# Step times per kind of batch: other places for a second half's projections and gates, a norm, a score maximum and the next batch's input

## The chip, the cores and the metric

The kernel runs on one core of a Trainium2 chip. The metric is the device time of one execution in microseconds; the median of three runs is compared. On the core, five engines work side by side, each through its own fixed list of instructions: TensorE (PE in the profile, its weight loads PEld), VectorE (DVE), ScalarE (ACT), GpSimd (POOL), and SyncE (SP), which issues transfers. They meet only at semaphores.

## The reference

Four batches of 1024 tokens of width 128 pass through four stages, each followed by a residual sum and a layer norm:

```python
x = _layernorm(x + _L0_attn_ref(x, ...))   # 8 heads, silu, rotary-like angles, exp mask, rms norm, gate
x = _layernorm(x + _L0_ffn_ref(x, ...))    # 2 layers: window attention over 64+64 keys, then gelu feed-forward
x = _layernorm(x + _L1_attn_ref(x, ...))   # 33 interpolated samples per token at computed positions, weighted
x = _layernorm(x + _L1_ffn_ref(x, ...))    # 8 experts, top 2 of a softmax over the tokens
```

The third stage computes, for each token, a frequency and a phase from two small projections (`wave`), 33 positions `pos`, and sums the rows at `floor(pos)` and the next one with weights from a third projection (`kernel`).

## The kernel before

A batch has a **first half** (the first two stages) and a **second half** (the third). The second half of batch b runs beside the first half of batch b+1, woven into it, and the experts' stage runs beside and behind the second half of batch 3. Everything in 128-token tiles t = 0 to 7 or in blocks j = 0, 1 of 512 tokens. In float32 a matmul shows as two records in the profile.

The first half's steps, by the names that `first` knows: the **opening** (`xT` transposes the loaded input, `kq` 0 to 7 are key and query projections with a Silu on ACT and a rotation on DVE, then `vu`, `kt`, `u`, `KV`, four pairs `E`/`heads` of masked scores, `square`, `rms`, `y`, `ao`, and the norms `mean`/`var` 0 and 1), then for two layers and eight tiles `proj`, `rn`, `rot`, `turn`, `v`, `S` (scores; on DVE their maximum), `X` (exp), `P`, `O`, `oT`, and by block `wo`, `mean`/`var`, three `ff` steps (gate and up projections, Gelu on ACT, product on DVE), and `down`. `shift` copies a block with half of its channels moved by a token. Norms 6 and 7 close the first half of blocks 0 and 1. So `ff(1,1,0)`, `ff(1,1,1)`, `ff(1,1,2)`, `down(1,1)`, `var(7)` are its last steps.

The second half: `x2t` j transposes the block, which SP writes to a table in memory, `wk` t is the projection of tile t, `pos` j the positions and gates of a block (on ACT a Silu, a Sigmoid and a Tanh with the tables that they need; on DVE eleven small instructions); `w` weights, then 88 chunks `g`: POOL gathers three times 128 rows, DVE multiplies them by weights (L1235), PE sums them by transposing into a bank (`acc`, L1612). Six chunk buffers go round. `wk` 4 to 7, `x2t` 1 and `co` share the one bank `c1`; `xT`, `kq`, norms, projections and feed-forward take turns in the two banks `pa` and `pb`, in program order.

What sets the order: no planner runs; `schedule(e)` writes each engine's list by **sorting the steps by a time**, a table value plus the batch's offset (`FIRST_AT`, `SECOND_AT`, a batch every 27.61 units) and a phase of the engine (`AT`). PE's list is also that of SP and POOL. A step in front that waits holds all behind it on that engine. The input of batch b+1 is loaded by SP in its `xT` step (L630), behind the store of the second half's last block (L658), which waits for DVE's `co` 1.

```python
def schedule(e):
    out = []
    for b in range(B):
        out += [(FIRST_AT[b] + time, ("first", b, *step)) for time, step in first_times(e)]
        out += [(SECOND_AT[b] + time, ("second", b, *step)) for time, step in second_times() if b < B - 1 or time < TAIL_AT]
    return [step for _, step in sorted(out, key=lambda x: x[0])] + tail_steps()
```

Of the kernel before, what the change touches and what calls it, by code (L numbers as in the profile page):

```python
# [79 lines left out]
FIRST_AT = (0.0, 27.61, 55.22, 82.83)  # L80
SECOND_AT = (0.0, 27.61, 55.22, 82.83)
TAIL_AT = 21.94
SECOND_LAYER = 9.0
OPENING_AT = (-10.02, -8.96, -8.18, -7.82, -7.49, -7.26, -7.09, -6.96, -6.78, -6.42, -6.24, -6.23, -5.49, -4.17, -3.83, -3.72, -3.41, -3.27, -3.2, -2.79, -2.78, -2.77, -2.76, -2.75, -2.49, -2.42, -2.27, -2.26, -2.25, -2.24, -2.23, -2.22, -2.19, -2.18, -2.13, -0.83)
DENSE_AT = ((5.59, 5.61, 5.89, 6.03, 6.23, 6.61), (9.33, 9.57, 9.81, 9.82, 10.54, 10.77), (14.63, 14.84, 15.16, 15.84, 16.08, 16.75, 17.15, 17.74), (18.22, 18.4, 18.45, 19.2, 19.51, 19.63, 20.16, 20.81))
HEAD_AT = ((17.93, 17.99, 18.0, 18.13, 18.14, 18.21, 19.38), (21.23, 21.24, 22.92, 23.7, 24.34, 25.36))
CHUNK = (0, 8, 9, 30, 45, 60, 75, 88)
CHUNK_AT = (19.61, 21.76, 23.16, 28.75, 33.26, 37.56, 41.27, 45.64)
SUM_LAG = 0.42
AT = {  # L90
# [9 lines left out]
def norm_steps(m):  # L100
    return [("mean", m), ("var", m)]


# [4 lines left out]
def opening_steps():

    steps = [("zero",), ("xT",)] + [("kq", i) for i in range(2 * J * G)] + [("vu",), ("kt",), ("u",), ("KV",), ("E", 0), ("E", 1), ("heads", 0), ("E", 2), ("heads", 1)]  # L110
    steps += [("square", 0), ("E", 3), ("heads", 2), ("rms", 0), ("heads", 3), ("y", 0), ("square", 1), ("ao", 0), ("rms", 1), ("mean", 0), ("y", 1), ("var", 0), ("ao", 1)]
    return steps + [("mean", 1), ("shift", 0, 0), ("var", 1), ("shift", 0, 1)]


def first_times(e):

    at = AT[e]
    out = [(time + at["opening"], step) for time, step in zip(OPENING_AT, opening_steps())]
    for l in range(LAYERS):
        for what, phase in at.items():  # L120
            if what not in ("wo", "opening", "dense"):
                out += [(SECOND_LAYER * l + t + phase, (what, l, t)) for t in range(T)]
        for j in range(J):
# [113 lines left out]
def tail_steps():  # L237

    late = second_head(1)
    done = {step for time, step in second_times() if time < TAIL_AT}  # L240
# [24 lines left out]
    return [("moe", B, "load")] + second[:h] + merge(second[h:k], [("moe", B, *x) for x in beside]) + second[k:] + [("moe", B, *x) for x in behind]  # L265
# [1578 lines left out]
```

## Time and profile before

| | |
|---|---|
| median of 3 runs (lowest to highest) | 1969.92 us (1968.27 to 1970.03) |
| the profiled execution, span | 2353.6 us |
| mean granted TensorE clock in it | 0.854 |
| busy: PE, DVE, ACT, POOL | 1720.4, 1254.1, 988.0, 1103.7 us |
| one batch's period | some 512 us |

The profiled execution has no time of its own beside its span, which begins with the first instruction and ends with the last. It took 1.195 times the median of the runs, so a time read from it stands for 0.837 of that in a run, if the stretch is like the rest. Starts are in microseconds from the span's start. A wait in square brackets is the idle time of the engine ahead of the instruction and who ended it.

### The profile page before, as it was taken

How to read it: one execution, taken by the hardware profiler on the slowest of the kernel's cores; microseconds unless marked ns; L12 is line 12 of the kernel's file. 1: busy time of each engine (PE TensorE's matmuls, PEld its weight loads, DVE VectorE, ACT ScalarE, POOL GpSimd, SP SyncE). 2: the span in 40 equal slices, each digit the busy share in tenths (PEclk: the TensorE clock that was granted, in tenths of full speed). 3: DMA queues.
4: the chain of work that ended last, by engine and by line, in shares of the span. 5: the costliest groups of instructions: out<-in, count | busy, mean ns of one | idle time of the engine just before them, and what ended most of it. 6: DMA issues, size and time to landing. Idle time of an engine off the chain costs nothing.

```text
span 2353.6 us, 31786 instructions
## 1 busy us (share of the span) xinstructions
PE 1720.4 (73%) x12145; PEld 1141.7 (49%) x12153; DVE 1254.1 (53%) x2158; ACT 988.0 (42%) x2363; POOL 1103.7 (47%) x1069
## 2 busy tenths in 40 slices
PE   5787876767777766666776766667787768879866
PEld 3354534445445534344555434454455346656645
DVE  6565645555556444555565545655565454343345
ACT  3365673234543551243353540335354533343333
POOL 0000016475556345664556255554665367766630
PEclk8799998778989877988898978789888879989876
DMA  3010023132223232232223232232233343223321
GB/s 133 10 24 14 19 48 96 58 102 83 79 75 103 63 74 79 79 96 73 88 79 90 56 95 70 83 90 72 86 89 85 69 148 99 88 81 90 88 47 36
DMA packets 93420, 178.72 MB, mean 76 GB/s; under 512 B 21452, under 2 KB 50264, under 8 KB 93016
## 3 DMA queue, kind: packets, MB, share of 16 engines
q0 software_dynamic: 50688, 138.48, 21.4%
q1 hardware_dynamic: 42584, 38.23, 5.8%
q8 instruction: 98, 1.61, 0.3%
q14 instruction: 50, 0.41, 0.1%
HBM read 151.46 MB, written 9.44 MB: 68 GB/s over the span
## 4 chain that ended last, share of the span: by engine, by line
PE 39%; DVE 19%; another core or an unknown queue 18%; ACT 12%; issue 9%; SPq 1%; POOL 1%; DMA 1%; DVEq 0%; POOLq 0%; ACTq 0%
PE c L1612 5%; DVE pool_c L1235 4%; PE pa L1508 3%; PE pb L1508 3%; PE ta L1542 2%; DVE ssq L1132 2%; PE ta L1516 2%; ACT pool_a L771 2%; ACT pool_a L836 2%; PE sc L1587 2%; DVE pool_a L1155 1%; DVE pool_a L1185 1%; PE tb L1389 1%; PE pb L1560 1%
## 5 line engine op out<-in xcount | busy, mean ns | idle before, releaser
L729 POOL DMA_INDIRECT pool_c<-rows_of_x,idx x1056 | 1100.9, 1043 | 1156.5 <-PE c L1612 380.0
L1612 PE MATMUL c<-ident,pool_c 128*128 128x128 f32 x2112 | 337.1, 303 | 61.6 <-DVE pool_c L1235 32.2
L1612 PEld LDWEIGHTS c<-ident,pool_c 128*128 128x128 f32 x2112 | 278.3, 158 | 143.0 <-issue 97.0
L1235 DVE TENSOR_TENSOR pool_c<-pool_c 128x768 f32<-128x768 f32 x352 | 331.3, 951 | 20.1 <-DMA pool_c<-rows_of_x,idx 19.7
L860 ACT ACTIVATE prob<-sc,nmax 128x128 f32<-128x128 f32 x512 | 179.3, 374 | 0.1
L1516 PE MATMUL ta<-ident,pool_a 128*128 128x128 f32 x512 | 90.9, 333 | 90.8 <-DVE pool_a L1155 80.4
L771 ACT COPY pool_a<-tb 128x512 f32<-128x512 f32 x188 | 112.5, 599 | 103.6 <-remote 58.3
L1155 DVE TENSOR_TENSOR pool_a<-ta,rinv 128x512 f32<-128x512 f32 x64 | 44.3, 692 | 199.9 <-remote 158.3
L1542 PE MATMUL ta<-vmix,pool_a 128*64 128x64 f32 x1024 | 80.9, 239 | 81.0 <-ACT pool_a L771 67.5
L1142 DVE TENSOR_REDUCE nmax<-sc 128x8 f32<-128x1024 f32 x64 | 77.5, 1211 | 103.9 <-remote 96.1
L1508 PE MATMUL pa<-wqkv,pool_a 128*128 128x512 f32 x192 | 118.8, 706 | 12.9 <-DVE pool_a L1185 7.4
L1516 PEld LDWEIGHTS ta<-ident,pool_a 128*128 128x128 f32 x512 | 74.6, 173 | 108.5 <-DVE pool_a L1155 87.6
L1508 PE MATMUL pb<-wqkv,pool_a 128*128 128x512 f32 x192 | 115.5, 687 | 13.3 <-DVE xm L1160 6.3
L1542 PEld LDWEIGHTS ta<-vmix,pool_a 128*64 128x64 f32 x1024 | 73.0, 152 | 101.7 <-issue 101.7
L860 ACT ACTIVATION_READ_ACCUMULATOR prob<-sc,nmax 128x1 f32 x512 | 109.8, 214 | 0.0
L836 ACT ACTIVATE pool_a<-pb 128x512 f32<-128x512 f32 x64 | 38.2, 597 | 168.7 <-PE pb L1508 100.1
L836 ACT ACTIVATE pool_a<-pa 128x512 f32<-128x512 f32 x64 | 38.2, 597 | 164.9 <-PE pa L1508 100.5
L1132 DVE TENSOR_REDUCE ssq<-pool_a 128x16 f32<-128x1024 f32 x64 | 77.9, 1218 | 43.9 <-ACT pool_a L836 42.0
L1542 PE MATMUL ta<-vring,pool_a 128*64 128x64 f32 x1024 | 82.3, 241 | 0.0
L1516 PE MATMUL tb<-ident,pool_a 128*128 128x128 f32 x512 | 77.8, 299 | 4.5 <-issue 4.4
L1199 DVE TENSOR_TENSOR pool_a<-pool_a,rot 128x1024 f32<-128x1024 f32 x64 | 78.4, 1225 | 2.2
L1196 DVE TENSOR_TENSOR pool_a<-pool_a,rot 128x1024 f32<-128x1024 f32 x64 | 78.1, 1220 | 2.8 <-remote 2.2
(413 smaller groups left out, 3344.3 us busy)
## 6 DMA issues: line engine op xcount, KB each, us to landing
pool_c<-rows_of_x,idx POOLq DMA_INDIRECT x1056
vmix<-vring SPq DMA_DIRECT2D x128, 128.0 KB
rows_of_x<-x2tok SPq DMA_DIRECT2D x16, 256.0 KB
xtok<-in_x SPq DMA_DIRECT2D x4, 512.0 KB
x_of_all<-x2tok SPq DMA_DIRECT2D x8, 256.0 KB
out<-pool_c SPq DMA_DIRECT2D x8, 256.0 KB, 2.3
wqkv<-in_wqkv SPq DMA_DIRECT2D x1, 1536.0 KB
xtok<-x_of_all SPq DMA_DIRECT2D x3, 512.0 KB
```

The costliest lines, as they stand in the source:

```text
L729: pool.indirect_dma_start(gat[:, n % GB, s, :], None, tables[b % 2], bass.IndirectOffsetOnAxis(ap=idx[:, t, SC * c + s:SC * c + s + 1], ax ...
L771: nc.scalar.copy(dst, src[:, :] if view is None else view(src)).then_inc(empty(key, b), 1)
L836: nc.scalar.activation(sq[:, w, :], src[:, :], ACT.Square).then_inc(SEM["b_square"], 1)
L860: ins = nc.scalar.activation(prob[:, n % 2, pr, e, :], sc[:, e, P * pr:P * (pr + 1)], ACT.Exp, bias=nmax[:, n % 2, e, pr:pr + 1], accum_ou ...
L1132: V.tensor_reduce(ssq[:, t % 2, 0, :], sq[:, :, :].rearrange("p w (h d) -> p (w h) d", h=HB), AXX, ALU.add).then_inc(SEM["b_ss"], 1)
L1196: V.tensor_tensor(r2.rearrange("p w h (s d) -> p w h s d", s=2), bass.AP(tensor=own.tensor, offset=own.offset + 32, ap=[own.ap[0], [INNER, ...
L1199: V.tensor_tensor(own.rearrange("p w (h d) -> p w h d", h=HB), own.rearrange("p w (h d) -> p w h d", h=HB), ap3(rot[:, l, t, 0, 0, :], [[D ...
L1235: V.tensor_tensor(g4, g4, wv, ALU.mult).then_inc(SEM["c_prod"], 1)
L1508: mm(out[:, :], hT[:, P * n:P * (n + 1)], wqkv[:, l, c:c + INNER], start=True, stop=True).then_inc(full(key, b), 1)
L1516: ins = mm(out[:, P * (k % PAIRS):P * (k % PAIRS + 1)], x, ident[:], start=(k == 0), stop=(k == len(parts) - 1), is_transpose=True, skip_g ...
L1542: ins = mm(out[q, DH * (2 * pr + e):DH * (2 * pr + e + 1)], PT[:, n % 2, pr, e, q], v[:, 2 * pr + e, :], start=True, stop=True, skip_group ...
L1612: ins = mm(out[:, c:c + P], x, ident[:], start=(i == 0 and k == 0), stop=(i == BCH - 1 and k == len(parts) - 1), is_transpose=True, skip_g ...
```

## The change

The tables get one version for each kind of batch: `KIND` sends batch 0 to version 0, batches 1 and 2 to version 1, batch 3 to version 2. Only times change, so each engine executes the same steps; ACT loads its function tables four times less (112 loads instead of 116). SP and POOL have the same lists as before. The diff, cut (`OPENING_AT`, `DENSE_AT` and `CHUNK_AT` have a row for each kind as `HEAD_AT` has):

```diff
@@
-HEAD_AT = ((17.93, 17.99, 18.0, 18.13, 18.14, 18.21, 19.38), (21.23, 21.24, 22.92, 23.7, 24.34, 25.36))
+KIND = (0, 1, 1, 2)
...
+HEAD_AT = (
+    ((17.93, 17.99, 18.0, 18.13, 18.14, 18.21, 19.38), (21.23, 21.24, 22.31, 25.46, 25.96, 26.48)),
+    ((17.93, 17.99, 18.0, 18.13, 18.14, 18.21, 19.31), (20.95, 21.17, 22.31, 25.46, 26.02, 26.34)),
+    ((17.93, 17.99, 18.0, 18.13, 18.14, 18.21, 19.38), (20.96, 21.23, 22.31, 25.46, 26.02, 26.31)),
+)
...
-    "pe": {"dense": 0.01, "proj": -1.95, "P": 1.06, "O": 1.27, "turn": -0.55, "v": -0.28, "oT": 1.72, "opening": -0.14, "S": -0.12, "wo": 1.9},
+    "pe": {"dense": 0.01, "proj": -1.95, "P": 1.06, "O": 1.24, "turn": -0.55, "v": -0.28, "oT": 1.72, "opening": -0.14, "S": -0.14, "wo": 1.91},
...
-def first_times(e):
+def first_times(e, b):
...
-    out = [(time + at["opening"], step) for time, step in zip(OPENING_AT, opening_steps())]
+    out = [(time + at["opening"], step) for time, step in zip(OPENING_AT[KIND[b]], opening_steps())]
...
-def second_times():
+def second_times(b):
...
-        out += list(zip(HEAD_AT[j], second_head(j)))
+        out += list(zip(HEAD_AT[KIND[b]][j], second_head(j)))
```

The numbers of the second row of `HEAD_AT` are the times of `x2t` 1, `wk` 4 to 7 and `pos` 1. Lines of the changed file from `tail_steps` on are 18 higher.

**PE, end of the first half of batch 1 and start of batch 2.** Before: `var(5)` (L1501), `ff(1,1,0)` (two of L1560), `xT` (two of L1389), `ff(1,1,1)`, `kq` 0 (L1405), `ff(1,1,2)`, `down(1,1)` (L1569), `kq` 1.

```order
L1501 MATMUL pa<-lnq,meanw 128x512
L1560 MATMUL pb<-pool_a,w 128x512
L1560 MATMUL pa<-pool_a,w 128x512
L1389 MATMUL pb<-ident,xtok 128x128 x4
L1389 MATMUL pa<-ident,xtok 128x128 x4
L1560 MATMUL pb<-pool_a,w 128x512
L1560 MATMUL pa<-pool_a,w 128x512
L1405 MATMUL pb<-xin,wkq 128x512
L1560 MATMUL pa<-pool_a,w 85x512
L1560 MATMUL pb<-pool_a,w 85x512
L1569 MATMUL pa<-up,w 128x512 x3
L1405 MATMUL pb<-xin,wkq 128x512
```

The same place in the change:

```order
L1519 MATMUL pa<-lnq,meanw 128x512
L1407 MATMUL pb<-ident,xtok 128x128 x4
L1407 MATMUL pa<-ident,xtok 128x128 x4
L1578 MATMUL pb<-pool_a,w 128x512
L1578 MATMUL pa<-pool_a,w 128x512
L1578 MATMUL pb<-pool_a,w 128x512
L1578 MATMUL pa<-pool_a,w 128x512
L1578 MATMUL pb<-pool_a,w 85x512
L1578 MATMUL pa<-pool_a,w 85x512
L1423 MATMUL pb<-xin,wkq 128x512
L1587 MATMUL pa<-up,w 128x512 x3
L1423 MATMUL pb<-xin,wkq 128x512
```

`xT` has moved ahead of all three `ff` steps and `kq` 0 behind them; it is so between batches 2 and 3 too, and not between 0 and 1. ACT's and DVE's lists follow. Behind this piece, `var(7)` moves from behind `kq` 6 to behind `kq` 3 on PE, and `x2t` 1 and `wk` 4 to ahead of `vu`.

**DVE, opening of batch 2.** Before: the last product of mask and scores (L1065) of `E` 0, a chunk product (L1235), `wk` 6 (L1213), the four of `E` 1, two chunk products.

```order
L1065 TENSOR_TENSOR pool_a<-tb,emask 128x512
L1235 TENSOR_TENSOR pool_c<-pool_c 128x768
L1213 TENSOR_TENSOR pool_c<-c,cb 128x280
L1065 TENSOR_TENSOR pool_a<-pa,emask 128x512
L1065 TENSOR_TENSOR pool_a<-pb,emask 128x512
L1065 TENSOR_TENSOR pool_a<-ta,emask 128x512
L1065 TENSOR_TENSOR pool_a<-tb,emask 128x512
L1235 TENSOR_TENSOR pool_c<-pool_c 128x768 x2
```

In the change:

```order
L1083 TENSOR_TENSOR pool_a<-tb,emask 128x512
L1253 TENSOR_TENSOR pool_c<-pool_c 128x768
L1083 TENSOR_TENSOR pool_a<-pa,emask 128x512
L1083 TENSOR_TENSOR pool_a<-pb,emask 128x512
L1083 TENSOR_TENSOR pool_a<-ta,emask 128x512
L1083 TENSOR_TENSOR pool_a<-tb,emask 128x512
L1253 TENSOR_TENSOR pool_c<-pool_c 128x768
```

`wk` 6 is gone from here and each chunk product stands one `E` earlier (the second one of the pair did). On PE, `wk` 6 leaves its place behind `E` 0, `wk` 7 its place behind `heads` 1, and the sums `acc` 10 and 11 move ahead of `E` 1. All three openings of batches 1 to 3 have it.

**ACT, norms and first projection of batch 2.** Before: `var(0)` (L823, L825), `pos` 1 of batch 1 with three table loads (L894 to L767), `mean(1)` (L818), `var(1)`, `proj` (L836).

```order
L823 ACTIVATE lnq<-pa,cols 128x512
L825 ACTIVATE lnq<-lnq 128x512
L894 ACT_TABLE_LOAD
L894 ACTIVATE pool_c<-pool_c 128x1120
L896 ACT_TABLE_LOAD
L896 ACTIVATE pool_c<-pool_c 128x32
L897 ACTIVATE pool_c<-pool_c 128x32
L767 ACT_TABLE_LOAD
L818 ACTIVATE lnq<-lnc 128x512
L823 ACTIVATE lnq<-pb,cols 128x512
L825 ACTIVATE lnq<-lnq 128x512
L836 ACTIVATE pool_a<-pa 128x512
```

In the change:

```order
L836 ACTIVATE lnq<-lnc 128x512
L854 ACTIVATE pool_a<-pb 128x512
L854 ACTIVATE pool_a<-pa 128x512
L860 ACTIVATE ssq<-ssq 128x16
L862 ACTIVATE ssq<-ssq,cols 128x16
L841 ACTIVATE lnq<-pb,cols 128x512
L843 ACTIVATE lnq<-lnq 128x512
L912 ACT_TABLE_LOAD
L912 ACTIVATE pool_c<-pool_c 128x1120
L914 ACT_TABLE_LOAD
L914 ACTIVATE pool_c<-pool_c 128x32
L915 ACTIVATE pool_c<-pool_c 128x32
```

`mean(1)`, the projection's squares and `rn` now stand ahead, then `var(1)`, then `pos` 1. On DVE `pos` 1 moves from between `shift(0,0)` and `var(1)` to behind `rot(0,0)`, `shift(0,1)` from behind `proj(0,1)` to behind `rot(0,1)`, and `wk` 6 and 7 stand between the first tile's steps. For batch 3, ACT has `pos` 1 ahead of `var(1)`.

Elsewhere, in the second layer, DVE has a chunk product ahead of some score maxima (tiles 1 to 3) that stood behind them, and PE and ACT have the tile-6 `P` ahead of `ff(1,0,1)`. In all, 59 chunk products stand ahead of a step of the first half that stood ahead of them.

## Rows read from the trace of the kernel before

**Rows 1.** The page: span, busy time of each engine, chain that ended last.

```profile
span 2353.6 us, 31786 instructions
...
PE 1720.4 (73%) x12145; PEld 1141.7 (49%) x12153; DVE 1254.1 (53%) x2158; ACT 988.0 (42%) x2363; POOL 1103.7 (47%) x1069
...
PE 39%; DVE 19%; another core or an unknown queue 18%; ACT 12%; issue 9%; SPq 1%; POOL 1%; DMA 1%; DVEq 0%; POOLq 0%; ACTq 0%
...
L1235 DVE TENSOR_TENSOR pool_c<-pool_c 128x768 f32<-128x768 f32 x352 | 331.3, 951 | 20.1 <-DMA pool_c<-rows_of_x,idx 19.7
```

**Rows 2.** All waits: engine, line, released by: us in total, times, longest.

```profile
POOL pool_c L729 <- PE c L1612: 380.0, 104, 13.8
...
DVE pool_a L1155 <- remote: 158.3, 35, 6.5
...
DVE pool_c L1235 <- DMA pool_c<-rows_of_x,idx: 19.7, 7, 4.7
```

**Rows 3.** Timeline, batches 1 to 2: start, us, engine, line, tiles, [idle before <- releaser].

```profile
844.38 0.51 SPq L630 DMA_DIRECT2D xtok<-in_x  x1
...
846.79 0.72 ACT L828 ACTIVATE pool_a<-lnc,cols 128x512 f32<-128x512 f32 x1 [0.82 <-DVE lnc L1113]
...
853.34 0.70 PE L1389 MATMUL pb<-ident,xtok 128*128 128x128 f32 x4 [2.40 <-DMA xtok<-in_x]
...
858.61 0.75 DVE L1166 SCALAR_TENSOR_TENSOR up<-pa,cols,lnq 128x512 f32<-128x512 f32 x1 [6.88 <-PE pa L1560]
...
862.84 1.28 ACT L880 ACT_TABLE_LOAD   x1
...
864.24 0.68 ACT L880 ACTIVATE lnc<-pa,cols 85x512 f32<-85x512 f32 x1
...
865.91 5.28 PE L1569 MATMUL pa<-up,w 128*128 128x512 f32 x6 [1.95 <-DVE up L1166]
```

**Rows 4.** Timeline, the same place between batches 2 and 3.

```profile
1364.65 0.66 PE L1389 MATMUL pa<-ident,xtok 128*128 128x128 f32 x4 [1.85 <-DMA xtok<-in_x]
...
1377.88 2.90 PE L1569 MATMUL pb<-up,w 128*128 128x512 f32 x3 [4.06 <-DVE up L1166]
```

**Rows 5.** The six down matmuls alone: stretch, us, PE busy, PEld busy, PEclk, DMA.

```profile
865.80:872.00 6.20, 5.28 (x6) 1.85 (x6) 0.59 0.00 0
353.60:357.00 3.40, 2.81 (x6) 1.06 (x6) 1.00 0.54 122
```

**Rows 6.** Timeline, var(7) and the second half's transposes, batches 1 to 2.

```profile
884.95 0.69 DVE L1119 TENSOR_TENSOR xm<-lnc,lnq 128x512 f32<-128x512 f32 x1 [3.14 <-ACT lnq L825]
...
890.75 0.59 ACT L771 COPY x2tok<-c 128x512 f32<-128x512 f32 x1 [3.84 <-remote]
...
891.39 1.30 PE L1600 MATMUL c<-wc,xm 128*128 128x280 f32 x2 [2.37 <-ACT x2tok L771]
```

**Rows 7.** Timeline of PE and of DVE, the opening of batch 2.

```profile
925.76 0.55 PE L1446 MATMUL pa<-pool_a 32*128 32x128 f32 x1 [5.49 <-DVE pool_a L1065]
...
934.78 0.69 DVE L1065 TENSOR_TENSOR pool_a<-pa,emask 128x512 f32<-128x512 f32 x1 [2.65 <-PE pa L1446]
...
938.45 0.63 PE L1600 MATMUL c<-wc,xm 128*128 128x280 f32 x2 [1.01 <-issue]
```

**Rows 8.** Timelines of ACT, DVE and PE, first projection of batch 2.

```profile
965.04 0.63 ACT L818 ACTIVATE lnq<-lnc 128x512 f32<-128x512 f32 x1
...
964.67 0.22 DVE L1312 TENSOR_REDUCE pool_c<-pool_c 128x8 f32<-128x64 f32 x1
...
967.38 0.23 DVE L1323 TENSOR_SCALAR pool_c<-pool_c 128x132 f32<-128x132 f32 x1
...
968.87 1.52 PE L1508 MATMUL pa<-wqkv,pool_a 128*128 128x512 f32 x2
...
969.22 0.69 DVE L1111 TENSOR_TENSOR x<-lnc,lnq 128x512 f32<-128x512 f32 x1 [1.61 <-ACT lnq L825]
```

**Rows 9.** Timeline of DVE, a score maximum of the second layer.

```profile
1223.77 1.22 DVE L1142 TENSOR_REDUCE nmax<-sc 128x8 f32<-128x1024 f32 x1 [3.82 <-remote]
```

More of the change, by code:

```diff
@@ L83 @@
 SECOND_LAYER = 9.0
-OPENING_AT = (-10.02, -8.96, -8.18, -7.82, -7.49, -7.26, -7.09, -6.96, -6.78, -6.42, -6.24, -6.23, -5.49, -4.17, -3.83, -3.72, -3.41, -3.27, -3.2, -2.79, -2.78, -2.77, -2.76, -2.75, -2.49, -2.42, -2.27, -2.26, -2.25, -2.24, -2.23, -2.22, -2.19, -2.18, -2.13, -0.83)
-DENSE_AT = ((5.59, 5.61, 5.89, 6.03, 6.23, 6.61), (9.33, 9.57, 9.81, 9.82, 10.54, 10.77), (14.63, 14.84, 15.16, 15.84, 16.08, 16.75, 17.15, 17.74), (18.22, 18.4, 18.45, 19.2, 19.51, 19.63, 20.16, 20.81))
-HEAD_AT = ((17.93, 17.99, 18.0, 18.13, 18.14, 18.21, 19.38), (21.23, 21.24, 22.92, 23.7, 24.34, 25.36))
-CHUNK = (0, 8, 9, 30, 45, 60, 75, 88)
-CHUNK_AT = (19.61, 21.76, 23.16, 28.75, 33.26, 37.56, 41.27, 45.64)
+KIND = (0, 1, 1, 2)
+OPENING_AT = (
[3 rows of a table added]
+)
+DENSE_AT = (
[3 rows of a table added]
+)
+HEAD_AT = (
[3 rows of a table added]
+)
+CHUNK = (0, 8, 9, 30, 45, 60, 75, 88)
+CHUNK_AT = (
[3 rows of a table added]
+)
 SUM_LAG = 0.42
 AT = {
[1 row of a table removed]
[1 row of a table added]
     "act": {"dense": 0.12, "P": 1.17, "rn": -1.72, "X": 0.44, "turn": -0.48, "v": -0.17, "oT": 1.83, "opening": -0.06, "proj": -2.05},
[1 row of a table removed]
[1 row of a table added]
 }
@@ L128, in first_times @@
                 steps += norm_steps(6 + j)
-            out += [(time + at["dense"], step) for time, step in zip(DENSE_AT[J * l + j], steps)]
+            out += [(time + at["dense"], step) for time, step in zip(DENSE_AT[KIND[b]][J * l + j], steps)]
             if l == 0:
@@ L132, in first_times, with chunk_time @@
     return out
-def chunk_time(n):
+def chunk_time(b, n):
     k = max(i for i in range(len(CHUNK) - 1) if n >= CHUNK[i])
-    return CHUNK_AT[k] + (CHUNK_AT[k + 1] - CHUNK_AT[k]) * (n - CHUNK[k]) / (CHUNK[k + 1] - CHUNK[k])
-def second_times():
+    at = CHUNK_AT[KIND[b]]
+    return at[k] + (at[k + 1] - at[k]) * (n - CHUNK[k]) / (CHUNK[k + 1] - CHUNK[k])
+def second_times(b):
     lag = {"acc": SUM_LAG, "cT": SUM_LAG + 0.05, "co": SUM_LAG + 0.1}
@@ L145, in second_times @@
     for j in range(J):
-        out += list(zip(HEAD_AT[j], second_head(j)))
-    out.append((HEAD_AT[0][-1], ("w", 0)))
+        out += list(zip(HEAD_AT[KIND[b]][j], second_head(j)))
+    out.append((HEAD_AT[KIND[b]][0][-1], ("w", 0)))
     for what, *a in second_steps()[HEAD:]:
         if what not in ("x2t", "wk", "pos"):
-            out.append((chunk_time(when(what, *a)) + lag.get(what, 0), (what, *a)))
+            out.append((chunk_time(b, when(what, *a)) + lag.get(what, 0), (what, *a)))
     return out
@@ L157, in schedule @@
     for b in range(B):
-        out += [(FIRST_AT[b] + time, ("first", b, *step)) for time, step in first_times(e)]
-        out += [(SECOND_AT[b] + time, ("second", b, *step)) for time, step in second_times() if b < B - 1 or time < TAIL_AT]
+        out += [(FIRST_AT[b] + time, ("first", b, *step)) for time, step in first_times(e, b)]
+        out += [(SECOND_AT[b] + time, ("second", b, *step)) for time, step in second_times(b) if b < B - 1 or time < TAIL_AT]
     return [step for _, step in sorted(out, key=lambda x: x[0])] + tail_steps()
@@ L239, in tail_steps @@
     late = second_head(1)
-    done = {step for time, step in second_times() if time < TAIL_AT}
+    done = {step for time, step in second_times(B - 1) if time < TAIL_AT}
     second = [("second", B - 1, *x) for x in late + [x for x in second_steps() if x not in late] if x not in done]
```

11 rows, old and new, of tables (AT, CHUNK_AT, DENSE_AT, OPENING_AT) are left out of this document.

## The prediction, made before the changed kernel ran

> **What bounds the kernel now.** I read the page first. No engine is full: PE is busy 73% of the span, DVE 53%, and the chain that ended last spreads over PE, DVE, ACT and 18% that it can't assign [rows 1]. So the bound is the order of in-order lists: a step whose input is late holds every step behind it on its engine, and the others wait in turn. The waits come next. The largest, POOL's 380.0 us for PE's sums, says that the gathers run ahead and are held back by the buffers; DVE's chunk products wait for a gather only 7 times of 352, 19.7 us in all [rows 2]. Then I read the timeline, place by place, where the change moves something, for each engine's wait and who ended it.
>
> The profiled span is 1.195 times the median of the runs. I sum in profiled time and multiply by 0.837. A part of the excess is in waits "remote", such as the 158.3 us ahead of L1155 [rows 2], where PE's records end and the reader still idles; a gain that fills such a wait may be smaller in a run (rival B). A measurement tells no change below 0.2%, 3.9 us of a run, from noise.
>
> **The terms.** Negative is faster.
>
> *Term 1: `xT` ahead of all three `ff`, `kq` 0 behind them; twice.* The input's load is issued at 844.38 and `xT` starts at 853.34, 9.0 later, when it lands; `ff(1,1,0)` could start when ACT's copy ends at 847.51 [rows 3] and now has to stand behind `xT`. So it is 7 us later. But what counts is when `down(1,1)` starts. Before: `xT` 853.34, the second `ff`'s product on DVE ends at 858.61 + 0.75 = 859.36, so 6.0 behind `xT`'s start; then `kq` 0 with its own function table, the third `ff` behind the load at 862.84, and `down` at 865.91 [rows 3]. After: the first `ff` takes the second one's place and ends at 859.4; the other two follow with nothing between them. Each has four matmuls, of 2.81/6 = 0.47 us at a granted clock of 1.00 (2.4 GHz) and 5.28/6 = 0.88 at 0.59 [rows 5], so 1.9 to 3.5 each. `down` at 863.2 to 866.4, against 865.91: -2.7 to +0.5. Between batches 2 and 3 `xT` starts at 1364.65 and `down` at 1377.88 [rows 4]; 1364.65 + 6.0 and the same two give 1374.5 to 1377.7: -3.4 to -0.2. In the middle (2.7 each) -1.1 and -1.8. Taken: **-2.9** (ends -6.1 and +0.3). What lay beside the stretch before, gathers on POOL and few products on DVE, needs no PE; the covers for `kq` 0's Silu and rotation are now the `down` matmuls, 5.28 long; without them two passes over 128x512, as the copy's 0.72 [rows 3], would be added. ACT also loads four tables less, each 1.28 [rows 3]: that lies inside this term where it is on the path, and elsewhere beside other work.
>
> The row has a load of 1.28 at 862.84 and the next activation at 864.24, 0.12 behind its end [rows 3]. The Trainium skill, "ScalarE: Activation LUTs", section "What ACT_TABLE_LOAD costs", adds a drain of about 1380 ns to each load. By that rule four loads less would be an estimated 5.5 us better than by the rows, and the run about 1951; the trace shows no such time, and I leave it out.
>
> *Term 2: `var(7)`, `x2t` 1 and `wk` 4 earlier; twice.* Before, PE waits 2.37 for ACT's copy of the transposed block ahead of `wk` 4 [rows 6]; with other work between, that can go: -2.4 at best. But `var(7)`'s DVE part, which already waited 3.14 for ACT [rows 6], now stands ahead of `kq` 3's rotation, and the wait would hold that and all behind it: +3.1 at worst. PE reaches the variance sooner as well, so I take near the middle, -0.5: **-1.0** (ends -4.8, +6.2).
>
> *Term 3: the opening's `wk` 6 and 7 moved out, `acc` 10 and 11 into a hole; three times.* PE waits 5.49 for DVE's masked scores at 925.76, and DVE then waits 2.65 for PE's scores of `E` 1 at 934.78 [rows 7]. What the change takes from between them: the two projections, 0.63 each on PE [rows 7], and the sums, which now stand in the hole of 5.49. At least the two 0.63 go (-1.2), at most the whole 2.65 (-2.7). I take -2.0, since both reach the same wait: **-6.0** (ends -3.6, -8.1). Chunk product and sum lose nothing, they only stand earlier.
>
> *Term 4: `pos` 1 from ahead of `mean(1)` to behind it; three times.* ACT reaches `mean(1)` at 965.04, directly behind `pos` 1's last load, and DVE spends 964.67 to 967.61 on `pos` 1's eleven small instructions, then waits 1.61 for `var(1)` at 969.22 [rows 8]. The projection's matmuls are at 968.87 [rows 8]. With the norm ahead, up to 2.9 leaves the path; but the work is done later, where DVE is full with the first tiles, so the gain may be given back: 0 to -2.9. I take the wait of 1.61 less some 0.4 for a `wk` that now stands there, -1.2: **-3.6** (ends 0, -8.7). For batch 3 ACT keeps `pos` 1 ahead of `var(1)`; DVE's order still changes.
>
> *Term 5: chunk products ahead of score maxima.* In the second layer DVE idles 3 to 4 us ahead of such a maximum, at 1223.77 3.82 long [rows 9], and a product of 0.95 [rows 1] that stood behind it now stands in front: inside the idle time, if its rows are there. I count eight such places: at most 8 x 0.95 = 7.6. As the wait is one of the "remote" ones, half: **-3.8** (ends 0, -7.6).
>
> The tile-6 `P` ahead of `ff(1,0,1)` changes who waits by one step each, both with slack: nothing; if PE had none, one step's four matmuls, 1.9, per batch. SP's and POOL's lists are the same: they are passed by nothing, and no DMA is issued at another place, so the load of the input isn't earlier.
>
> Sum: -2.9 - 1.0 - 6.0 - 3.6 - 3.8 = -17.3, times 0.837 = -14.5 us: **1955**. All the best ends give -35.3 (1940), all the worst +2.9 (1972).
>
> **Rivals.**
>
> *B: the waits are partly the profiler's.* Then only work that leaves the way on its own engine counts: term 1's -2.9, term 3 at its small end -3.6, term 4 with the 0.44 saved thrice, -1.3; terms 2 and 5 nothing. -7.8, so 1963. For it: the factor 1.195 and the "remote" waits; against it: PE's wait of 5.49 and DVE's of 2.65 have plain releasers.
>
> *C: TensorE at its low clock.* Before, PE works on `ff(1,1,0)` while the input is on its way and waits 2.40 for it [rows 3]; after, it waits from the norm's variance on, longer than the 5.8 between the copy's end at 847.51 and 853.34. It is at 0.59 in `down` already, against 1.00 in the same six matmuls elsewhere, 5.28 against 2.81 [rows 5]. If the longer wait keeps it at 1.2 GHz for all of the `ff`s and for 10 us of work more, term 1 is at its worst (+3.2 against the sum) and the rest costs 5 each, 10 in two places: -17.3 + 13.2 = -4.1, so 1966; with 14 us of work at the low level in place of 10 nothing is left. Against it: one more `ff` then comes without a pause.
>
> The Trainium skill, "TensorE: Matmul & The Clock Gate", section "HAM oscillation — how this bites in real kernels", says that a matmul burst behind a wait for a DMA starts with the clock halved, every time. That speaks against `xT` first; this case's trace agrees as far as 0.59 behind such a wait goes, but the same clock stood there with the shorter wait, so by the trace the rule doesn't price the longer one.
>
> *D: slower, by gathers that are no longer ahead.* 59 chunk products stand ahead of a first-half step that they stood behind, with POOL's list unchanged. Where the rows haven't landed, DVE waits in front of the step. Now 7 of 352 wait, 2.8 each [rows 2]. It decides from an average of (17.3 + 4.7) / 59 = 0.37 per moved product; with one in five waiting, 12 x 2.8 = 34, the sum is +16 and the run 1984. Against it: POOL waits 380.0 us for buffers that PE frees [rows 2], so it's ahead nearly always; and earlier sums free buffers earlier. For it: in the opening the first gathers of a second half have only begun, and the sums' place there depends on them.
>
> **How the numbers follow.** Forecast 0.45, B 0.20, C 0.15, D 0.17, anything else 0.03. Faster by over 0.2%: nearly all of the forecast and of B, a quarter of C: 0.66. Within 0.2%: most of C, a little of the forecast and B: 0.16. Slower: D and the rest, 0.18. The time is the forecast's, 1955. The forecast's own range is 1944 to 1964 (terms 3 to 5 at their ends together: -25 or -8). The range of 8 in 10 takes in B, C and the worst ends of the unknown costs (1972) and ends where D begins: 1944 to 1974.
>
> **What the changed profile would show.** Term 1: `down(1,1)` 10 to 11 behind `xT`'s start, against 12.57 and 13.23; the first `ff` directly behind `xT`; no table load for `kq` 0 between the `ff`s. Term 2: no wait for `x2tok` ahead of `wk` 4; a DVE wait for ACT's `var(7)` over 3.1 ahead of `kq` 3 would show its bad end. Term 3: DVE's first product of `E` 1 without the 2.65, and the two sums inside PE's 5.49. Term 4: `var(1)` on DVE without the 1.61, the first projection sooner behind `var(0)`, and no new wait in the first tiles, where `pos` 1 now stands. Term 5: the wait ahead of the maximum of [rows 9] shorter by one product, not moved to PE. B: the same orders, waits "remote" shifted. C: a granted clock below 0.6 over `ff`, `down` and the `kq` behind, where the batch's period grows. D: the chunk products' wait for DMA well above 19.7 us.
>
> The prediction is wrong if the steps between the handovers aren't shortened because something behind them (the scores of the tiles, the sums that PE owes POOL) sets the period anyway: then each gain is a longer wait later, and the result lies within 0.2%.

## The result, and the profile after

The changed kernel took 1949.75 us (median of 4 runs, 1943.64 to 1954.63), the kernel before 1969.1 (4 runs); the ratio is 0.9904, 95% interval 0.9882 to 0.9927. Measured again (experiment e8) it was 0.994, 0.9917 to 0.9963; of the 30 runs of the kernel before beside it two took 2058.64 and 3894.19 us, none of the others over 1977, and these two are not in the ratios of e5 to e8. So the two measurements say 0.6 and 1.0% faster (their intervals go from 0.4 to 1.2%), and a difference below 0.2% can't be told from these runs.

The page of the changed kernel: span, busy time, and the groups of the gathers and of the chunk products.

```profile
span 1950.2 us, 31782 instructions
...
PE 1573.4 (81%) x12145; PEld 1058.5 (54%) x12153; DVE 1253.8 (64%) x2158; ACT 975.7 (50%) x2359; POOL 1111.7 (57%) x1069
...
L747 POOL DMA_INDIRECT pool_c<-rows_of_x,idx x1056 | 1108.8, 1050 | 747.0 <-issue 352.0
L1253 DVE TENSOR_TENSOR pool_c<-pool_c 128x768 f32<-128x768 f32 x352 | 332.7, 951 | 144.4 <-DMA pool_c<-rows_of_x,idx 143.7
```

This span agrees with the median, so it isn't stretched as a whole, as the one of [rows 1] was by 1.195. And the chunk products wait 143.7 us for gathered rows, where [rows 1] had 19.7. Read by itself that looks like a cost of the change. It took a second profile of the kernel before (experiment e1, span 1971.5) to read this rightly. Its waits (engine, line, released by: total, times, longest), those of POOL and of the chunk products:

```profile
POOL pool_c L729 <- PE c L1612: 76.5, 57, 9.1
...
DVE pool_c L1235 <- DMA pool_c<-rows_of_x,idx: 138.4, 84, 7.8
```

The same of the changed kernel:

```profile
POOL pool_c L747 <- PE c L1630: 63.8, 54, 9.5
...
DVE pool_c L1253 <- DMA pool_c<-rows_of_x,idx: 143.7, 82, 7.4
```

So in an undisturbed execution of the kernel before, POOL waits 76.5 us for PE's sums and not 380.0 [rows 2], and the rows are late 84 times and not 7. The change hardly moves that: 138.4 before, 143.7 after. In both kernels the engine with little slack is POOL. The changed kernel's batches 0 and 1, from the first to the end of the last of a batch's 264 gathers (stretch, us, POOL busy, PEclk, DMA, GB/s):

```profile
334.60:701.70 367.10, 279.67 (x264) 0.94 0.39 108
718.00:1099.90 381.90, 280.71 (x264) 0.92 0.38 106
```

279.7 busy and 263 times 0.30 between two gathers are 359 of 367: with few exceptions POOL issues one gather after the other. From the last gather of a batch to the first of the next another 16 us go by (701.7 to 718.0 here). So with the gathers as they are a period can't be below some 375 us, an estimate from these rows, and it is 380 to 400. What lies between is POOL's pauses, and a change of order can win them. I read them from POOL's timeline, gap by gap; chunks and batches are counted from 0, and "the pause at chunk 21" is the one behind that chunk's last gather, ahead of the first one of chunk 22. It is the largest in the middle of each batch of the kernel before. In e1, batch 1, and what PE did around it, with [rows 8] standing for the same place:

```profile
821.06 0.95 POOL L729 DMA_INDIRECT pool_c<-rows_of_x,idx  x1 [0.30 <-issue]
...
831.10 1.38 POOL L729 DMA_INDIRECT pool_c<-rows_of_x,idx  x1 [9.08 <-PE c L1612]
```

```profile
823.77 2.05 PE L1496 MATMUL pa<-x,meanw 128*128 128x512 f32 x2 [2.93 <-DVE x L1082]
827.47 2.08 PE L1501 MATMUL pb<-lnq,meanw 128*128 128x512 f32 x2 [1.65 <-ACT lnq L818]
829.34 1.49 PE L1612 MATMUL c<-ident,pool_c 128*128 128x128 f32 x6
```

PE waits for `mean(1)` and then for `var(1)`, in order, and the sum of chunk 16 stands behind both, though its product (L1235) began at 813.50. Chunk 22 goes into the buffer that chunk 16 leaves, as six buffers go round, so POOL's gather waits for that sum, 9.08 us. The same place in the changed kernel: two sums (L1630) stand between the mean of block 1 and the projection (L1526), and `var(1)` (L1519) comes behind.

```profile
811.72 1.10 PE L1514 MATMUL pa<-x,meanw 128*128 128x512 f32 x2 [2.06 <-DVE x L1100]
812.66 1.03 PE L1630 MATMUL c<-ident,pool_c 128*128 128x128 f32 x6
813.48 1.14 PE L1618 MATMUL c<-wc,xm 128*128 128x280 f32 x2
814.42 1.49 PE L1630 MATMUL c<-ident,pool_c 128*128 128x128 f32 x6
815.70 1.44 PE L1526 MATMUL pb<-wqkv,pool_a 128*128 128x512 f32 x2
```

No gather near it waits: the first one of chunk 22 starts at 815.78, with the usual 0.30 ahead of it. Counted over the 0.3 between gathers, the pauses at chunk 21 were 2.9, 8.8 and 8.5 us in batches 0 to 2 of e1, and none in the changed kernel. The pauses at chunk 5 (7.5 and 5.3 in batches 1 and 2 of e1, 9.2 and 8.3 after) and at chunks 62 to 68 (5 to 12 in a batch, in both) are still there.

Where the time went, by the start of each batch's first gather in the two profiles:

```
batch                        0       1       2       3    last gather ends    span
before (e1)              337.6   725.2  1124.4  1524.0        1878.9        1971.5
changed                  334.6   718.0  1115.4  1506.3        1859.2        1950.2
gained since column left   3.0     4.2     1.8     8.7           2.0           1.6
```

3.0 lies ahead of the first gather, where the orders hardly differ; in the thirteen undisturbed profiles of this case that start lies anywhere from 333.0 to 337.6. The rest, some 18, is gained behind it. It isn't the pauses' length batch by batch: batch 1 lost a pause of 8.8 and is only 1.8 shorter, as other pauses of it grew, by 1.7 at chunk 5 and by 5.1 at chunks 62 and 64.

### The profile page after: what moved, and what is told of

Read it like the earlier page. It is cut to its first block and busy times, and to the rows that moved or that the text cites. A ratio compares the mean times of both kernels' runs of the same rounds, so it can differ in the third digit from the quotient of the medians.

```text
span 1950.2 us, 31782 instructions
## 1 busy us (share of the span) xinstructions
PE 1573.4 (81%) x12145; PEld 1058.5 (54%) x12153; DVE 1253.8 (64%) x2158; ACT 975.7 (50%) x2359; POOL 1111.7 (57%) x1069
## 3 DMA queue, kind: packets, MB, share of 16 engines
q8 instruction: 98, 1.61, 0.3%
## 5 line engine op out<-in xcount | busy, mean ns | idle before, releaser
L1253 DVE TENSOR_TENSOR pool_c<-pool_c 128x768 f32<-128x768 f32 x352 | 332.7, 951 | 144.4 <-DMA pool_c<-rows_of_x,idx 143.7
L1630 PE MATMUL c<-ident,pool_c 128*128 128x128 f32 x2112 | 311.1, 287 | 57.8 <-DVE pool_c L1253 57.8
L1630 PEld LDWEIGHTS c<-ident,pool_c 128*128 128x128 f32 x2112 | 255.4, 148 | 139.6 <-DVE pool_c L1253 74.8
L1526 PE MATMUL pa<-wqkv,pool_a 128*128 128x512 f32 x194 | 106.6, 632 | 13.8 <-DVE pool_a L1203 8.9
L1526 PE MATMUL pb<-wqkv,pool_a 128*128 128x512 f32 x190 | 104.6, 633 | 9.3 <-DVE pool_a L1203 4.6
L1560 PE MATMUL ta<-vmix,pool_a 128*64 128x64 f32 x1024 | 72.0, 224 | 27.5 <-ACT pool_a L789 27.5
L1560 PEld LDWEIGHTS ta<-vmix,pool_a 128*64 128x64 f32 x1024 | 64.5, 138 | 47.8 <-issue 47.8
L1160 DVE TENSOR_REDUCE nmax<-sc 128x8 f32<-128x1024 f32 x64 | 76.7, 1198 | 13.8 <-PE sc L1605 13.8
L1534 PE MATMUL ta<-ident,pool_a 128*128 128x128 f32 x512 | 73.8, 291 | 11.1 <-DVE pool_a L1173 10.9
L1534 PEld LDWEIGHTS ta<-ident,pool_a 128*128 128x128 f32 x512 | 62.1, 150 | 21.6 <-DVE pool_a L1173 13.7
L958 ACT ACTIVATE prob<-prob 128x512 f32<-128x512 f32 x52 | 32.8, 631 | 81.1 <-DVE prob L1302 81.1
L1560 PE MATMUL ta<-vring,pool_a 128*64 128x64 f32 x1024 | 73.3, 225 | 0.0
```

The lines of the kernel that those rows point to most:

```text
L1160: V.tensor_reduce(nmax[:, n % 2], sc[:, :, :].rearrange("p e (r k) -> p e r k", r=PAIRS), AXX, ALU.max, negate=True).then_inc(SEM["b_max"], 1)
L1253: V.tensor_tensor(g4, g4, wv, ALU.mult).then_inc(SEM["c_prod"], 1)
L1526: mm(out[:, :], hT[:, P * n:P * (n + 1)], wqkv[:, l, c:c + INNER], start=True, stop=True).then_inc(full(key, b), 1)
L1534: ins = mm(out[:, P * (k % PAIRS):P * (k % PAIRS + 1)], x, ident[:], start=(k == 0), stop=(k == len(parts) - 1), is_transpose=True, skip_g ...
L1560: ins = mm(out[q, DH * (2 * pr + e):DH * (2 * pr + e + 1)], PT[:, n % 2, pr, e, q], v[:, 2 * pr + e, :], start=True, stop=True, skip_group ...
L1630: ins = mm(out[:, c:c + P], x, ident[:], start=(i == 0 and k == 0), stop=(i == BCH - 1 and k == len(parts) - 1), is_transpose=True, skip_g ...
```

## The experiments

Each kernel is timed against the kernel before on the same chip; ratios are to it, with 95% intervals. e1 to e4 ran on one chip, e5 to e8 on a second, e9 to e12 on a third; the changed kernel itself ran beside e5 to e7 alone (as e8), so elsewhere a kernel is compared with it by the ratios, 0.994 and 0.9904. Runs of one kernel spread by 0.5 to 1%, so differences between two ratios below about 0.3% are not read.

**e1, the kernel before again.** No edit.

> The kernel before, unchanged, for a second profile and for the spread of the comparison. If the first profile's stretched waits (span 1.195 times the median) belong to that one execution, this span is about 1967 us, the period of a batch about 400, and DVE's waits for gathered rows well above 19.7 us, since in the profile of the changed kernel they are 143.7. If they belong to the order of the steps before, the span stays above 2200. Ratio 1.000 within 0.003 by either.

1.0018 (0.9996 to 1.0041), span 1971.5, waits for rows 138.4. The stretching belonged to the one execution that the prediction was read from. The "remote" waits belonged to it too: 19 groups of waits end so there, and none in e1.

**e2 and e3, the order around `xT` alone, and all but it.**

```diff
 DENSE_AT, last row, kinds 1 (mean 5, var 5, ff x3, down; kinds 0 and 2 likewise)
-18.22, 18.4, 18.45, 19.2, 19.51, 19.63
+18.24, 18.4, 19.02, 19.14, 19.18, 19.49
```

> The kernel before with term 1 alone (the five times of the last feed-forward and its norm's start, all kinds of batch). By the terms of the prediction -2.9 x 0.837 = -2.4 us, so 1967 of 1969.5 (0.9988). By rival C (TensorE at its low level behind the longer wait for the input) nothing or up to +3: 1969 to 1972. If the handover is worth more than was summed, as the changed kernel's profile shows the last projection 2.1 and 2.9 us sooner behind the transposes with a full clock, up to -6: 1963.

> The changed kernel with term 1 undone (the same five times from the kernel before). By the terms 1949.8 + 2.4 = 1952 (0.9915 of before); by rival C 1950 or below (0.990); if term 1 carries a third of the gain, 1956 (0.9935).

e2: 1.0012 (0.9996 to 1.0027), no change; the 0.9988 of term 1 lies outside. e3: 0.995 (0.9929 to 0.9971), beside 0.994 and 0.9904 of the changed kernel. Term 1 brings nothing alone, and most of the gain is there without it. By e3 alone it could still carry a part in company with the others (its third reading, 0.9935, is inside the interval); e11, which has it undone as well and gives 0.9899, speaks against that. The profiles say why. `xT` and `down(1,1)` of the changed kernel and then of the undisturbed kernel before, in PE's timeline:

```profile
732.32 1.11 PE L1407 MATMUL pb<-ident,xtok 128*128 128x128 f32 x4 [8.41 <-DMA xtok<-in_x]
...
734.25 2.04 PE L1578 MATMUL pb<-pool_a,w 128*128 128x512 f32 x2
...
737.80 1.14 PE L1578 MATMUL pb<-pool_a,w 128*128 128x512 f32 x2
...
742.84 2.39 PE L1587 MATMUL pa<-up,w 128*128 128x512 f32 x5
```

```profile
740.25 0.66 PE L1389 MATMUL pb<-ident,xtok 128*128 128x128 f32 x4 [2.31 <-DMA xtok<-in_x]
...
741.63 2.08 PE L1560 MATMUL pb<-pool_a,w 128*128 128x512 f32 x2 [0.28 <-ACT xin L771]
...
749.65 2.81 PE L1569 MATMUL pa<-up,w 128*128 128x512 f32 x6 [1.78 <-DVE up L1166]
```

10.5 from `xT` to `down` was in the forecast (10 to 11). But before it is 9.4, not the 12.6 of [rows 3], and the six matmuls take 2.81 and not 5.28. Between batches 2 and 3 it is 8.2 before and 10.3 after. So from the start of `xT` the new order is one or two microseconds longer and not three shorter, and that isn't seen in the time.

**e4, terms 3 and 4 undone.**

```diff
 HEAD_AT, second row, kind 1 (x2t 1, wk 4 to 7, pos 1)
-(20.95, 21.17, 22.31, 25.46, 26.02, 26.34)
+(20.95, 21.17, 22.92, 23.7, 24.34, 25.36)
 and the times of the kernel before for the opening from u on, and CHUNK_AT
```

> The changed kernel with terms 3 and 4 undone: wk 5 to 7, pos 1, the opening's times from u on and the chunk times from the kernel before. By the terms 1949.8 + 9.6 x 0.837 = 1957.8 (0.9945). By rival B (only a wait's own work leaves) + (3.6 + 1.3) x 0.837 = 4.1: 1954 (0.9925). If the gathers pace the second half, so that only the places of pos 1 and of the first chunks matter, most of the 19 us go with it: 1963 or more (0.997).

1.004 (1.0021 to 1.0059), 1974.29: the whole gain is gone, and more, as by the third of the readings. POOL's pause at chunk 21 is back in all three batches (4.5, 5.7, 6.6 over the usual gap). Everything that the change does elsewhere (terms 1, 2 and 5 and the tile-6 `P`) is in this kernel and wins nothing. Batch 1 in POOL's timeline:

```profile
827.90 1.38 POOL L747 DMA_INDIRECT pool_c<-rows_of_x,idx  x1 [6.02 <-PE c L1630]
```

**e5, one cause on the kernel before.** Only the place of six chunks is changed, by 0.2 of the table's units (products, sums, and the weights of tile 2, which are timed by chunk 16); no projection, position or norm moves against another.

```diff
-    return at[k] + ...
+    return (-0.2 if 14 <= n < 20 else 0) + at[k] + ...
```

> The kernel before with one thing changed: products and sums of chunks 14 to 19 stand 0.2 table units earlier, so that the sum of chunk 16 comes ahead of the norms of block 1 on TensorE instead of behind them. Theory, gathers set the pace: GpSimd issues 264 gathers per batch, 1.05 us each and 0.30 between, some 357 of 397 us, and its pauses are what a batch can still lose; in the kernel before it pauses at chunk 21, 2.9, 8.8 and 8.4 us, for a buffer that the sum of chunk 16 frees. Then this alone takes up to 20 us: 1950 to 1957 of 1968. Rival, the norms and positions on VectorE are what was won (terms 3 and 4): their order is as before here, so 1966 to 1970.

0.9947 (0.9926 to 0.9968), 1957.81. This small edit has the size of the whole change as e8 measures it on the same chip (0.994), and a bit more than half of it by the first measurement (0.9904). The order of `var(1)`, `pos` 1 and the projections is the old one, so the rival of its expectation, 1966 to 1970, is out. The pause of batch 0 is gone, those of batches 1 and 2 are 4.9 and 1.6 and one chunk later, since the next sum (17) is still behind `var(1)`; batch 1 in POOL's timeline:

```profile
829.07 1.38 POOL L747 DMA_INDIRECT pool_c<-rows_of_x,idx  x1 [5.23 <-PE c L1630]
```

**e8, the changed kernel again.** No edit.

> The changed kernel as it is, on the same chip as the three others, for their baseline and for a second profile: ratio 0.990 within 0.003; GpSimd's pauses at chunk 5 (about 9 us) and at chunks 62 to 68 (about 10 us) of batches 1 and 2 again, none at chunk 21.

0.994 (0.9917 to 0.9963), 1953.53, a little outside the 0.990 within 0.003 that was expected; pauses at chunk 5 of 9.2 and 8.9, none at 21.

**e9, the counterpart on the changed kernel.** The sums of chunks 16 to 19 go back behind `var(1)`, on PE alone:

```diff
+            if what == "acc" and b < B - 1 and 16 <= a[0] < 20:
+                time = 26.33 + 0.001 * (a[0] - 16)
```

> The changed kernel with only TensorE's sums of chunks 16 to 19 moved back behind the variance of block 1 (var 1); VectorE's and ScalarE's lists stay as in the change. Gather theory: GpSimd pauses at chunk 21 or 22 again, by about what the sum of chunk 16 is late (some 10 us), rows of chunks behind it land late, and VectorE waits for them: 1962 to 1970, so most of the gain is lost by one move on one engine. Rival (the gain is in VectorE's order of norm, positions and projections): within 2 us of the changed kernel, 1950 to 1955.

1.0053 (1.0032 to 1.0073), 1978.77: slower than the kernel before, and beyond the 1962 to 1970 of its own theory. Four sums of 0.8 us at another place on one engine cost some 25 us (22 to 29 by the two ratios of the changed kernel). In the change `var(1)` stands later than before, so the sums behind it are later too: the pauses at chunk 21 are 8.5, 8.7 and 10.1, where e1 had 2.9 in batch 0. POOL in batch 0, then DVE, then all waits for rows:

```profile
430.52 0.94 POOL L750 DMA_INDIRECT pool_c<-rows_of_x,idx  x1 [8.79 <-PE c L1633]
```

```profile
443.90 0.96 DVE L1256 TENSOR_TENSOR pool_c<-pool_c 128x768 f32<-128x768 f32 x1 [0.98 <-DMA pool_c<-rows_of_x,idx]
...
448.64 0.96 DVE L1256 TENSOR_TENSOR pool_c<-pool_c 128x768 f32<-128x768 f32 x1 [1.38 <-DMA pool_c<-rows_of_x,idx]
...
456.60 0.96 DVE L1256 TENSOR_TENSOR pool_c<-pool_c 128x768 f32<-128x768 f32 x1 [0.82 <-DMA pool_c<-rows_of_x,idx]
...
461.84 0.96 DVE L1256 TENSOR_TENSOR pool_c<-pool_c 128x768 f32<-128x768 f32 x1 [3.20 <-DMA pool_c<-rows_of_x,idx]
```

```profile
DVE pool_c L1256 <- DMA pool_c<-rows_of_x,idx: 162.0, 92, 7.1
```

The chain can be read: a late sum, a full set of buffers, gathers 8.8 us later, and 13 to 31 us on, products of chunks 24 to 28 that wait for their rows with the first tiles' steps queued behind them on DVE. Beside the changed kernel's first profile, the score maximum of tile 0 is 1.8 later, of tile 1 5.2, of tile 2 8.7 (the batch was 0.6 early ahead of the sums), and in this batch the 9 stay to its end. At the three `down(1,1)` that follow, the lag is 9.2, 13.8 and 27.5 in all, so beside pauses of 8.5, 8.7 and 10.1 it grows by 9, 5 and 14.

**e10, term 3 undone alone.** `wk` 5 to 7, opening and chunk times from the kernel before, `pos` 1 and `var(1)` late as in the change.

```diff
 HEAD_AT, second row, kind 1
-(20.95, 21.17, 22.31, 25.46, 26.02, 26.34)
+(20.95, 21.17, 22.92, 23.7, 24.34, 26.34)
```

> The changed kernel with wk 5 to 7, the opening's times from u to mean 1 and the chunk times of the kernel before; positions and var 1 late as in the change. The terms of the prediction say +5 (6.0 x 0.837): 1957. Gather theory: the sum of chunk 16 stays ahead of var 1, as var 1 is late, so no pause at chunk 21 and at most the openings' own 2.4 us each come back: 1955 to 1958 too, and the profile without a pause at chunk 21 tells that the late var 1 is what lets the sum through.

0.9966 (0.9949 to 0.9984), 1960.97, 3 to 4 us above both forecasts. A third to a little over half of the gain is left; pauses at chunk 21 of 0.7, 3.1 and 1.0 instead of 2.9, 8.8 and 8.5. The time doesn't tell the two forecasts apart, only the profile does: with `var(1)` late, the sum passes, mostly. With e4 it splits the two terms: term 3 undone costs 5 to 12 us (0.994 or 0.9904 to 0.9966) where 5.0 was forecast, term 4 undone on top 14.6 (0.9966 to 1.004, from two chips) where 3.0 was forecast.

**e6 and e11, steps that seemed to gain nothing undone** (in e6 the times of `ff(1,0,1)` and `ff(1,0,2)`, which set the place of the tile-6 `P`; in e11 those of term 1 too).

```diff
 DENSE_AT, third row, kind 1 (ff(1,0,1), ff(1,0,2))
-16.08, 16.26
+15.84, 16.08
```

> The changed kernel with the steps ff(1,0,1) and ff(1,0,2) back at their times before, so that the feed-forward step stands ahead of P of tile 6 again. The prediction said that this costs nothing. By the first half's step times the changed kernel gives back 2.4, 1.0 and 1.0 us there: 4 us faster than the changed kernel, 1946. If only GpSimd's pauses count, its pauses at chunks 62 to 68 (6 to 12 us per batch) must get shorter for that; if they stay, no change, 1950.

> The changed kernel with both steps that its profile shows to gain nothing undone: the order around xT (term 1) and ff(1,0,1), ff(1,0,2). If the first half's step times count (0.5 and 2.0 us lost at the two handovers, up to 4 at the feed-forward steps), 4 to 6 us faster than the changed kernel, 1945 to 1948. If the two are free as e3 and e6 came out, 1950 to 1953.

0.9922 (0.9893 to 0.9951), 1949.44, and 0.9899 (0.9865 to 0.9934), 1951.37: neither can be told from the changed kernel. The 4 us that were read from the step times are neither shown nor excluded: e6's median is 4.1 below that of e8 on the same chip, with intervals of 0.3% on both.

**e7 and e12, the other pause.** Products and sums of the first chunks ahead of the wait for the input, three in e7, one in e12 (on e6).

```diff
+FIRST_CHUNKS = (18.41, 18.42, 18.43, 19.61, 19.92, 20.25, 20.6, 21.0, 21.4)
+FIRST_SUMS = (18.45, 18.46, 18.47)
...
+    if b in (1, 2) and n < len(FIRST_CHUNKS):
+        return FIRST_CHUNKS[n]
...
-    out.append((HEAD_AT[KIND[b]][0][-1], ("w", 0)))
+    out.append((18.4 if b in (1, 2) else HEAD_AT[KIND[b]][0][-1], ("w", 0)))
```

> The changed kernel with the weights and products of the first three chunks of the second halves 1 and 2 placed ahead of the wait for the next batch's input, their sums on TensorE too, and chunks 3 to 8 spread over the places of 2 to 8. GpSimd pauses 9.2 and 8.3 us at chunk 5 in the changed kernel, as all six buffers are full until the first sum. If the gathers set the pace, most of these pauses go: 12 to 15 us faster than the changed kernel, 1935 to 1938. If the first half's steps set the pace, three products and sums ahead of the transposes cost up to 1 us per batch: 1950 to 1952.

> The changed kernel with ff(1,0,1) and ff(1,0,2) back, and one chunk's product and sum (with the weights) ahead of the wait for the input; in e7 the second and third products waited 4.7 and 2.2 us for their rows and pushed the transposes 5 us back, the first waited for nothing. GpSimd's pause at chunk 5 falls from 9 to under 5 us and the transposes stay where they are. If that pause costs time, 6 to 10 us faster than the changed kernel, 1941 to 1945. If rows that come sooner are not needed sooner, as GpSimd's next pauses grow instead, no more than e6: 1947 to 1950.

e7: 0.9966 (0.9944 to 0.9988), 1960.70, 7 us above its neighbour e8 and outside both of its readings. The pause at chunk 5 is gone, but in its place DVE waits for rows ahead of the steps at the handover, where one batch's first half ends and the next one's begins:

```profile
729.64 1.03 DVE L1260 TENSOR_TENSOR pool_c<-pool_c 128x768 f32<-128x768 f32 x1
735.39 0.96 DVE L1260 TENSOR_TENSOR pool_c<-pool_c 128x768 f32<-128x768 f32 x1 [4.72 <-DMA pool_c<-rows_of_x,idx]
738.55 0.96 DVE L1260 TENSOR_TENSOR pool_c<-pool_c 128x768 f32<-128x768 f32 x1 [2.21 <-DMA pool_c<-rows_of_x,idx]
```

`xT` then starts at 740.90, 5 us late against the changed kernel's handover (the batch itself was 3.4 late already). This is rival D, made by hand: a product ahead of its rows holds the step behind it. In e12 the first pause comes one chunk later and is half as long, in batch 1:

```profile
752.48 1.30 POOL L754 DMA_INDIRECT pool_c<-rows_of_x,idx  x1 [4.64 <-PE c L1637]
```

e12: 0.9894 (0.9867 to 0.9921), 1948.57. It is the fastest median of all, but its interval holds 0.9904: not told apart from the changed kernel. So a pause of POOL does not cost its length everywhere. Part of the reason can be read: idle time taken away early partly comes back. Both kernels have new pauses of 1.6 to 2.6 ahead of chunks 17 to 22, and all pauses of a kernel together are 49 us in e7 against 56 in e8, though 18 were removed at chunk 5, and 48 in e12 against 50 in e6, though 8 were. The other part is a reading that no run tests: at chunk 5 the rows that come later are for products that stand behind the opening's work on DVE; at chunk 21 they are needed within some 15 us.

**All profiles side by side.** From the first gather of batch 1 to the first one of batch 3, in the thirteen undisturbed profiles:

| | pause at chunk 21 or 22, batches 1 and 2 | the two batches, us |
|---|---|---|
| e1, e2, e4, e9 | 5.7 to 10.1 | 798.7, 800.1, 802.2, 807.1 |
| the changed kernel, e8, e3, e6, e11 | none | 788.3, 794.8, 782.4, 786.8, 786.3 |
| e5, e7, e10, e12 | 1.0 to 4.9 | 788.4, 793.2, 786.7, 779.6 |

Every kernel with the long pause is slower there than every other. But the nine others spread over 15 us, and one batch without the pause (batch 1 of e8, 399.5) is as long as the same batch of e1 with it (399.1).

## Why the prediction came out right, and where it wasn't

The direction, the time (1955 forecast, 1949.75) and the range hold. That the sum came out near is luck: its terms have the wrong weights, one of them carries most of the gain by a mechanism that the prediction doesn't have, and the reading of what bounds the kernel was wrong. (The forecast's own range, 1944 to 1964, is also not what its terms give: terms 3 to 5 at their ends make -28.3 and -7.5, which is 1946 to 1964.)

**What bounds the kernel.** "The gathers run ahead" was the step that failed. It rested on 380.0 and on 7 waits [rows 2], from a stretched execution: PE busy 1720.4 us [rows 1] against 1590.5 in e1, while POOL's busy time is the same within 12 us; as I read it, that left POOL time to get ahead. e1 shows 76.5 and 84. Multiplying by 0.837 repairs a sum of durations, not a reading of who waits for whom. And one row was in the stretched trace too: at 969.35 the gather waits 10.81 for a sum, right at the place of [rows 8]. I took it for POOL being ahead, as all the others.

**Term 1**, -2.4 of a run: measured as nothing (e2, e3). The changed order went as stated, at 10.5; what was wrong is the distance before it, a stretched 12.6 that is 9.4 in e1. So there was nothing to win, and the clock had a part in what was lost (rival C).

**Term 2**, -0.8. Not measured alone. The wait for `x2tok` ahead of `wk` 4 is gone, as forecast. In its place DVE waits 3.33 ahead of `var(7)`'s last step (3.14 in [rows 6]), now between the early `kq` steps, and a `kq` matmul of PE then 2.19 for its bank; e4 has it all and gains nothing.

**Terms 3 and 4**, -8.0 together: e4 against the changed kernel 1.004 to 0.994 (or 0.9904), 20 to 27 us. The sum was mis-sized by a factor of two and a half or more, most of it in term 4 (14.6 for 3.0, by e4 and e10), and the mechanism was another. Term 3 was also misread: the wait of 2.65 at 934.78 [rows 7] is the one ahead of `E` 2, and `E` 1's, at 927.91, is 1.07. Undisturbed the waits that I priced are smaller (in e1 1.90 for the 2.65, 0.67 for the 1.61 of [rows 8]), so by the theory of the terms the gain should have been smaller. The opening did get shorter by what term 3 says: from the first product of `E` 0 to that of `E` 3 it is 15.1 to 16.1 in e1 and 13.3 to 13.9 in the changed kernel. But e5, whose opening keeps its 16, is level with e8, so these 2 us a batch are not what the time shows. "Chunk product and sum lose nothing, they only stand earlier": that was it. With `pos` 1 and `var(1)` late, and the sums earlier, the sum of chunk 16 passes ahead of `var(1)` and POOL's buffer comes free in time; e5 moves only chunks and has the gain, e9 moves four sums back and loses more than it.

**Term 5**, -3.2: not seen. The maxima's group waited 7.2 us in all 64 in e1 and 13.8 after; the 3.82 of [rows 9] was a stretched wait, and there was next to no idle time to fill. From the maximum of tile 0 to that of tile 7 in the second layer it is 110.1, 110.3 and 110.0 in e1, and 110.5, 110.1 and 110.0 in e6, which has the moved products and not the moved tile-6 `P`.

**The tile-6 P**, 0: open. In the changed kernel tile 7's maximum comes 1 to 3 us sooner (109.1, 108.4 and 106.8 for the distances above), but `down(1,1)` starts 58.4 behind it and not 54.7 as in e6 (batch 1). The three kernels without the move have 0.9922, 0.9899 and 0.9894 (e6, e11, e12), the three with it 0.9904, 0.994 and 0.995 (the changed kernel twice, e3): that leans to a cost of some microseconds, with intervals that overlap.

**Rivals.** B was right that the waits "remote" were not real (e1 has none), and wrong on the sum. C: behind the wait of 8.41 for the input the granted clock is 0.50 over the next 5.5 us (732.3 to 737.8) and 0.98 over the 7.5 behind them; in e1, behind a wait of 2.31, it is 0.64 over 3.5 us and then 0.95. So the longer wait did leave a longer slow stretch, but `down` runs at full rate in both (2.39 for five of its six records), not at 0.59, and what it costs is of the size of the one or two microseconds above. C's 10 us of slow work more didn't come here. The Trainium skill ("TensorE: Matmul & The Clock Gate", section "HAM oscillation — how this bites in real kernels") has each burst behind a wait of several microseconds for a DMA start at half speed; the trace agrees for the first matmuls, 2.04 for a pair at 734.25 and 1.14 from 737.80 on, the levels of 1.2 and 2.4 GHz. But in e1, with the shorter wait of 2.31, the pair behind `xT` took 2.08 as well: by the first pair the rule doesn't tell the two orders apart. D named the right resource with the wrong sign: the moved sums free the buffers that POOL's gathers need, and earlier sums free them earlier, which the text had as a half sentence "against it". Its sign, waits for rows well above 19.7 (143.7), came true in the kernel before as well (138.4), so it says nothing of the change.

## What to carry to other kernels

Compare a profile's span with the timed runs first; if they differ as here, by 20%, take another profile before asking who waits for whom: in the stretched one POOL, which is just short of the bound, looked as if it waited for PE. When a ring of buffers couples a steady producer (here 264 gathers per batch, 359 of 367 us) to in-order lists, the place of the step that frees a buffer can matter more than that of the steps that compute: look for gaps in the producer and at what the releasing step stands behind. And a gap does not count by its length alone: 8.5 to 10.1 us at chunk 21 went with 5 to 14 us a batch (e9), and 4 to 9 at chunk 5, once removed, brought nothing that can be measured (e7, e12), partly as other gaps grew.

## What was not expected

One execution of the kernel before took 2353.6 us, with waits between PE's records where nothing is recorded, while the second profile, with the same orders, has 1971.5. What stretched it is not explained here. A gather took 1.05 us of POOL in both kernels, and 0.30 lay between two in any place, so that 22% of POOL's time in a batch (79 of 359) is neither busy nor waiting for anything shown.
